# One block of every 16-step turn fetched by SP, row by row: a GRU over a projected embedding table

## The chip, the cores and the metric

The kernel runs on one core of one Trainium2 chip. The metric is the device time of one execution in microseconds (us). Three runs of the kernel before took 1089.58, 1090.4 and 1093.35 us; the median is 1090.4 us. The engines of the core are named as in the profile: PE (TensorE, matrix products and transposes), PEld (its weight loads), DVE (VectorE), ACT (ScalarE), POOL (GpSimd) and SP (SyncE, here used to issue DMAs). Each engine has its own instruction queue, and they wait for each other through semaphores.

## The reference

A batch of 512 sequences of 200 item numbers goes through a gated recurrent unit with 128 hidden features, and the last state is classified into 100 classes:

```
x   = emb[item_seq]                      # emb: 12500 x 128, float32
mx  = x_t @ W + b_i ;  mh = h @ U + b_r  # W, U: 128 x 384
z   = sigmoid(mx[:, :D] + mh[:, :D])
r   = sigmoid(mx[:, D:2D] + mh[:, D:2D])
hh  = tanh(mx[:, 2D:] + r * mh[:, 2D:])
h   = where(item_seq_t != 0, z*h + (1-z)*hh, h)     # 200 steps in order
y   = softmax(h_last @ Wout + bout)
```

Item numbers may lie past the end of the table; they are brought into its rows first.

## The kernel before

**The table.** Since x_t @ W depends on the item alone, the kernel first multiplies the whole embedding table by W and stores the product in HBM as `table`: one row of 384 float32 values (1536 bytes) for each item. It also stores the transposed embedding itself as `rows` (512 bytes each). The last stores of the table are issued by SP (L226 to L230).

**The steps.** The batch is cut into four blocks of 128 sequences. Blocks 0 and 1 form chain 0, blocks 2 and 3 form chain 1; the chains are independent, and PE, ACT and DVE work on them in turn, so that one chain's matrix products lie beside the other's gates. The first 10 steps (`RAW`) use rows of the plain embedding, gathered while the table is still being made. The other 190 steps, numbered n = 0 to 189 (step t is n + 10), use rows of the table.

**The gathers.** For each step and block POOL issues one indirect DMA (L302) that fetches 128 rows of `table` into the arena, a ring of 12 steps in SBUF; the row numbers lie in `row_table` in SBUF, one for each partition. That is 4 gathers a step and 760 in all, written out one after the other. Before a chain's gathers of step n, POOL waits until PE has transposed the rows of step n - 12 out of the same slot (`s_free`).

**PE.** In each table step and chain PE transposes the gathered rows into the gates' sums in PSUM (`transpose_rows`, L377, six transposes), waiting for each block's slot semaphore, and then adds h @ U (L383, L385, L389). DVE's last instruction of a step and chain is L552, which makes the new h. The table steps run in a loop on PE, ACT and DVE whose body is one turn of the ring: with a ring of 12, 15 turns and 10 steps left over.

**SP.** Once the table is stored, SP has nothing to do until the result (L233).

Of the kernel before, what the change touches and what calls it, by code (L numbers as in the profile page):

```python
# [7 lines left out]
I32 = mybir.dt.int32  # L8
# [4 lines left out]
P = 128  # L13
# [2 lines left out]
CHAINS = ((0, 1), (2, 3))  # L16
WIDTH = 2 * P
RAW = 10
RING = 12
CHUNK = 8  # L20
HALF = CHUNK // 2
GROUP = 4
# [1 line left out]
AHEAD = 4  # L24
# [3 lines left out]
def gru(nc: bass.Bass, item_seq, emb_cols, W, U, b_i, b_r, Wout, bout, out):  # L28
# [14 lines left out]
    BATCH, STEPS = item_seq.shape  # L43
# [3 lines left out]
    assert D == P and GATES == 3 * D and BATCH == BLOCKS * P and 1 <= RAW <= RING  # L47
    TURNS = (STEPS - RAW) // RING
    LEFT = STEPS - RAW - TURNS * RING
    BOTH = range(len(CHAINS))  # L50

    TILES = ITEMS // P
# [7 lines left out]
    rows = nc.dram_tensor("rows", [ITEMS + 1 + P, D], F32, kind="Internal").ap()  # L60
    row_tiles = rows[0:TILES * P, :].rearrange("(p j) n -> p j n", j=TILES)
    table = nc.dram_tensor("table", [ITEMS + 1 + P, GATES], F32, kind="Internal").ap()
    table_tiles = table[0:TILES * P, :].rearrange("(p j) n -> p j n", j=TILES)

    with ExitStack() as ctx:
# [3 lines left out]
        def sem(name):  # L69
            return ctx.enter_context(nc.semaphore(name))  # L70

        def per_chain(name):
            return [sem(f"{name}{c}") for c in BOTH]

# [92 lines left out]
        s_padrow = sem("pad_rows_stored")  # L167

        s_slot = [[sem(f"slot{s}_block{k}_gathered") for k in range(BLOCKS)] for s in range(RING)]
        s_x = per_chain("x_turned")  # L170
        s_xT = per_chain("xT_ready")
        s_free = per_chain("rows_transposed")
# [18 lines left out]
        def over_table_steps(eng, one_turn):  # L191
            with eng.Fori(0, TURNS) as turn:
                one_turn(turn, RING)
            one_turn(TURNS, LEFT)

        def columns(i):
            return arena[:, i * P:min((i + 1) * P, ITEMS)]

        @block.sync
        def _(sp):  # L200
            for q in range(CHUNKS):
                sp.dma_start(arena[:, q * CHUNK * P:(q + 1) * CHUNK * P],
                             emb_cols[:, q * CHUNK * P:(q + 1) * CHUNK * P]).then_inc(s_emb[q], 16)
            sp.dma_start(arena[:, CHUNKS * CHUNK * P:ITEMS], emb_cols[:, CHUNKS * CHUNK * P:ITEMS]
                         ).then_inc(s_emb[CHUNKS], 16)

            for q in range(CHUNKS):
                sp.wait_ge(s_tact, q + 1)
                sp.wait_ge(s_tdve, q + 1)
                sp.dma_start(row_tiles[:, q * CHUNK:(q + 1) * CHUNK, :], turned[q % STAGES][:, :, :]  # L210
                             ).then_inc(s_rows[q % STAGES], 16)
            sp.wait_ge(s_tact, CHUNKS + 2)
            sp.wait_ge(s_tdve, CHUNKS + 1)
            sp.dma_start(row_tiles[:, TILES - 1, :], turned_last[:, 0, :]).then_inc(s_rows_last, 16)
            sp.dma_start(rows[TILES * P:ITEMS, :], turned_last[0:REST, 1, :]).then_inc(s_rows_last, 16)
            sp.dma_start(rows[ITEMS + 1:ITEMS + 1 + P, :], turned_last[:, 2, :]).then_inc(s_rows_last, 16)

            for g in range(GROUPS):
                sp.wait_ge(s_pact, (g + 1) * (GROUP // 2))
                sp.wait_ge(s_pdve, (g + 1) * (GROUP // 2))  # L220
                sp.dma_start(table_tiles[:, g * GROUP:(g + 1) * GROUP, :], proj[g % AHEAD][:, :, :]
                             ).then_inc(s_store[g % AHEAD], 16)
            last = proj[GROUPS % AHEAD]
            s_last = s_store[GROUPS % AHEAD]
            sp.wait_ge(s_pact, GROUPS * (GROUP // 2) + 1)
            sp.dma_start(table_tiles[:, TILES - 1, :], last[:, 0, :]).then_inc(s_last, 16)  # L226
            sp.wait_ge(s_pdve, GROUPS * (GROUP // 2) + 1)
            sp.dma_start(table[TILES * P:ITEMS, :], last[0:REST, 1, :]).then_inc(s_last, 16)
            sp.wait_ge(s_pact, GROUPS * (GROUP // 2) + 2)
            sp.dma_start(table[ITEMS + 1:ITEMS + 1 + P, :], last[:, 2, :]).then_inc(s_last, 16)  # L230

            sp.wait_ge(s_prob, 1)
            sp.dma_start(out.rearrange("(k p) n -> p k n", p=P), probs[:, :, :]).then_inc(s_out, 16)  # L233
            sp.wait_ge(s_out, 16)

        @block.gpsimd
        def _(pool):
            pool.memset(ident[:, :], 0.0).then_inc(s_ident0, 1)
            pool.memset(pins[:, :], 0.0).then_inc(s_ident0, 1)
            pool.wait_ge(s_ident0, 1)  # L240
            pool.affine_select(out=ident[:, :], in_=ident[:, :], compare_op=ALU.not_equal, fill=1.0,
                               base=0, pattern=[[-1, P]], channel_multiplier=1).then_inc(s_ident, 1)
            pool.wait_ge(s_ident0, 2)
            pool.affine_select(out=pins[:, :], in_=pins[:, :], compare_op=ALU.not_equal, fill=PINNED,
                               base=0, pattern=[[-1, P]], channel_multiplier=1).then_inc(s_pins, 1)

            pool.iota(copy_i[:, :], pattern=[[1, 1]], base=2, channel_multiplier=1).then_inc(s_copy, 1)
            pool.wait_ge(s_copy, 1)  # L250
            pool.tensor_copy(copy_f[:, :], copy_i[:, :]).then_inc(s_copy, 1)
            pool.wait_ge(s_seq, 16)
            pool.tensor_copy(item_f, seq[:, :, :]).then_inc(s_idx, 1)
            pool.wait_ge(s_idx, 1)
            pool.wait_ge(s_copy, 2)
            pool.tensor_scalar(over_f, item_f, float(ITEMS), copy_f[:, 0:1], ALU.is_ge, ALU.mult
                               ).then_inc(s_copy, 1)
            pool.tensor_scalar(row_f, item_f, 0.0, float(ITEMS), ALU.is_lt, ALU.mult).then_inc(s_idx, 1)
            pool.wait_ge(s_idx, 2)
            pool.tensor_tensor(row_f, row_f, item_f, ALU.add).then_inc(s_idx, 1)  # L260
            pool.tensor_scalar(pad_f, item_f, 0.0, float(ITEMS), ALU.is_equal, ALU.mult).then_inc(s_idx, 1)

            pool.tensor_scalar(masked[:, :].rearrange("p (t k) -> p t k", k=BLOCKS),
                               item_f[:, :, 0:RAW].rearrange("p k t -> p t k"), 0.0, None, ALU.is_equal
                               ).then_inc(s_pins, 1)
            pool.wait_ge(s_idx, 4)
            pool.tensor_scalar(row_f, row_f, 0.0, float(ITEMS - 1), ALU.max, ALU.min).then_inc(s_idx, 1)
            pool.wait_ge(s_idx, 5)
            pool.tensor_tensor(row_f, row_f, pad_f, ALU.add).then_inc(s_idx, 1)
            pool.wait_ge(s_idx, 6)  # L270
            pool.wait_ge(s_copy, 3)
            pool.tensor_tensor(row_f, row_f, over_f, ALU.add).then_inc(s_idx, 1)
            pool.wait_ge(s_idx, 7)
            pool.tensor_copy(row_table[:, :, :], row_f.rearrange("p k t -> p t k")).then_inc(s_idx, 1)
            pool.wait_ge(s_idx, 8)
            pool.wait_ge(s_pins, 2)

            pool.wait_ge(s_padrow, 16 * 2)
            for q in range(STAGES):
                pool.wait_ge(s_rows[q], 16 * len(range(q, CHUNKS, STAGES)))  # L280
            pool.wait_ge(s_rows_last, 16 * 3)
            for t in range(RAW):
                for k in range(BLOCKS):
                    pool.indirect_dma_start(  # L284
                        raw_row(t, k), None, rows,
                        bass.IndirectOffsetOnAxis(row_table[:, t, k:k + 1], 0)
                    ).then_inc(s_slot[t][k], 16)

            for q in range(AHEAD):
                stores = len(range(q, GROUPS, AHEAD)) + (3 if q == GROUPS % AHEAD else 0)  # L290
                pool.wait_ge(s_store[q], 16 * stores)
            for t in range(RAW, STEPS):
                n = t - RAW
                s = n % RING
                for c in BOTH:
                    if n >= RING:

                        pool.wait_ge(s_free[c], n - RING + 1)
                    for k in CHAINS[c]:
                        if n < RAW:  # L300
                            pool.wait_ge(s_slot[n][k], 16)
                        pool.indirect_dma_start(  # L302
                            ring_rows(s, k), None, table,
                            bass.IndirectOffsetOnAxis(row_table[:, t, k:k + 1], 0)
                        ).then_inc(s_slot[s][k], 16)

        @block.tensor
        def _(pe):
# [59 lines left out]
            def transpose_rows(turn, s, c):  # L368

                t = RAW + turn * RING + s  # L370
                for i, k in enumerate(CHAINS[c]):
                    for n, (dst, g) in enumerate(((reset_sum[c], 1), (cand_x[c], 2), (update_sum[c], 0))):
                        if n == 0:
                            pe.wait_ge(s_slot[s][k], turn * 16 + (32 if s < RAW else 16))
                        if n == 2 and i == 0:
                            pe.wait_ge(s_z[c], t)
# [233 lines left out]
```

## Time and profile before

| | before |
|---|---|
| median of three runs | 1090.4 us |
| profiled execution | 1093.43 us |
| its span, first to last instruction | 1091.6 us |
| PE busy | 981.0 us (90%) |
| DVE busy | 862.6 us (79%) |
| POOL busy | 803.7 us (74%) |
| POOL gathers of the table (L302) | 760, 979 ns each |
| granted TensorE clock, mean | 0.991 |

The span is the time between the first and the last instruction of the profiled execution; 1.8 us of its own time lie around it, and it took 3.0 us more than the median of the runs. Busy times of engines add up to more than the span, since the engines work side by side. "Idle before" is the time an engine stood still just before an instruction, and what ended that is inferred from semaphore events, so it can be named wrongly.

### The profile page before, as it was taken

To read this page: it belongs to the slowest core of one execution; us is meant where nothing else is said; L and a number is where in the kernel's file an instruction comes from. 1 tells how busy PE (TensorE), PEld (TensorE's weight loads), DVE (VectorE), ACT (ScalarE), POOL (GpSimd) and SP (SyncE) were. 2 spreads that over 40 slices of the span, in tenths; PEclk is the share of its full clock that TensorE was granted. 3 is DMA by queue.
4 is the path that set the end of the run, shared out by engine and by line. 5 is a ranking of instruction groups with operands and counts; after the bars stand their busy time and mean duration, and the time that the engine had idled before them with its cause. 6 is when DMAs were issued, how large, how long until landed. Compare 5 with 4: busy or idle time off the path is not lost.

```text
span 1091.6 us, 15880 instructions
## 1 busy us (share of the span) xinstructions
PE 981.0 (90%) x5185; PEld 756.4 (69%) x5185; DVE 862.6 (79%) x2074; ACT 577.7 (53%) x1288; POOL 803.7 (74%) x820
## 2 busy tenths in 40 slices
PE   6899999999999999999999999888888888888885
PEld 5556887777777777777777776666666666666664
DVE  3344778888888888888888888888888888888886
ACT  3334655555555555555555555555555555555554
POOL 6574777777777777777777777777777777777773
PEclk9899999999999999999999999999999999999998
DMA  9997555555555555555555555555555555555552
GB/s 359 378 360 262 159 157 153 153 152 154 151 155 152 153 153 153 154 152 152 153 156 152 153 152 154 153 152 151 154 152 155 153 153 154 153 152 154 152 155 81
DMA packets 59696, 185.75 MB, mean 170 GB/s; under 512 B 14830, under 2 KB 16408, under 8 KB 59672
## 3 DMA queue, kind: packets, MB, share of 16 engines
q0 software_dynamic: 49920, 152.09, 49.4%
q1 hardware_dynamic: 8356, 32.47, 7.5%
q10 hardware_dynamic: 1396, 0.91, 0.3%
q8 instruction: 9, 0.15, 0.1%
q14 instruction: 15, 0.12, 0.0%
HBM read 159.35 MB, written 26.07 MB: 170 GB/s over the span
## 4 chain that ended last, share of the span: by engine, by line
DVE 29%; DMA 23%; PE 16%; issue 12%; ACT 11%; POOL 9%; DVEq 0%; SPq 0%; POOLq 0%; ACTq 0%
DMA arena<-table,row_table 21%; ACT cand L482 10%; DVE rh L541 10%; POOL arena L302 9%; DVE zc L549 9%; DVE pre L544 9%; PE bank L318 5%; PE bank L377 4%; DMA rows<-turned 1%; PE bank L383 1%; DVE h L552 1%; PE bank L389 1%; PE bank L385 1%; PE bank L358 1%; PE bank L362 1%
## 5 line engine op out<-in xcount | busy, mean ns | idle before, releaser
L302 POOL DMA_INDIRECT arena<-table,row_table x760 | 744.4, 979 | 241.0 <-issue 178.2
L377 PE MATMUL bank<-ident,arena 128*128 128x128 f32 x2280 | 346.5, 277 | 64.3 <-DMA arena<-table,row_table 63.9
L377 PEld LDWEIGHTS bank<-ident,arena 128*128 128x128 f32 x2280 | 269.4, 141 | 141.6 <-DMA arena<-table,row_table 103.0
L482 ACT ACTIVATE cand<-pre,bi 128x256 f32<-128x256 f32 x400 | 203.3, 508 | 280.4 <-DVE pre L544 280.4
L383 PE MATMUL bank<-h,U_sb 128*128 128x256 f32 x800 | 261.6, 409 | 22.5 <-DVE h L552 4.9
L549 DVE SCALAR_TENSOR_TENSOR zc<-z,cand 128x256 f32<-128x256 f32 x400 | 171.2, 428 | 92.9 <-ACT cand L482 92.9
L389 PE MATMUL bank<-h,U_sb 128*128 128x256 f32 x800 | 239.3, 381 | 0.0
L385 PE MATMUL bank<-h,U_sb 128*128 128x256 f32 x800 | 238.6, 380 | 0.0
L478 ACT ACTIVATE r<-bank,b_gates 128x256 f32<-128x256 f32 x400 | 185.1, 463 | 83.3 <-PE bank L383 82.2
L541 DVE SCALAR_TENSOR_TENSOR rh<-bank,br,r 128x256 f32<-128x256 f32 x400 | 191.8, 479 | 44.6 <-ACT r L478 34.2
L480 ACT ACTIVATE z<-bank,b_gates 128x256 f32<-128x256 f32 x400 | 189.3, 473 | 69.8 <-PE bank L389 69.8
L552 DVE TENSOR_TENSOR h<-zh,zc 128x256 f32<-128x256 f32 x400 | 172.9, 432 | 13.8
L544 DVE TENSOR_TENSOR pre<-rh,bank 128x256 f32<-128x256 f32 x400 | 168.2, 420 | 13.8
L383 PEld LDWEIGHTS bank<-h,U_sb 128*128 128x128 f32 x800 | 120.1, 190 | 74.0 <-DVE h L552 73.9
L546 DVE TENSOR_TENSOR zh<-z,h 128x256 f32<-128x256 f32 x400 | 169.7, 424 | 0.4 <-ACT z L480 0.4
L385 PEld LDWEIGHTS bank<-h,U_sb 128*128 128x128 f32 x800 | 152.4, 190 | 20.7
L389 PEld LDWEIGHTS bank<-h,U_sb 128*128 128x128 f32 x800 | 137.3, 190 | 37.6 <-DVE pre L544 3.1
L318 PE MATMUL bank<-W_sb,arena 128*128 128x384 f32 x198 | 70.5, 510 | 3.7 <-ACT proj L453 3.7
L318 PEld LDWEIGHTS bank<-W_sb,arena 128*128 128x128 f32 x198 | 38.6, 201 | 28.5 <-ACT proj L453 4.4
L517 DVE COPY proj<-bank 128x384 f32<-128x384 f32 (+1 forms) x49 | 27.2, 557 | 39.0 <-PE bank L318 33.7
L284 POOL DMA_INDIRECT raw<-rows,row_table x40 | 38.0, 950 | 20.2 <-issue 11.9
L453 ACT COPY proj<-bank 128x384 f32<-128x384 f32 x50 | 23.8, 479 | 45.0 <-PE bank L318 39.1
(55 smaller groups left out, 165.8 us busy)
## 6 DMA issues: line engine op xcount, KB each, us to landing
table<-proj SPq DMA_DIRECT2D x24, 768.0 KB, 3.9
arena<-table,row_table POOLq DMA_INDIRECT x760, 3.1
arena<-in_L_rec_emb SPq DMA_DIRECT2D x12, 512.0 KB, 10.1
rows<-turned SPq DMA_DIRECT2D x12, 512.0 KB, 10.7
raw<-rows,row_table POOLq DMA_INDIRECT x40, 4.0
seq<-in_r_item_seq ACTq DMA_DIRECT2D x1, 400.0 KB, 10.3
table<-proj SPq DMA_DIRECT2D x2, 192.0 KB
out_probs<-probs SPq DMA_DIRECT2D x1, 200.0 KB, 2.6
```

The lines of the kernel that those rows point to most:

```text
L302: pool.indirect_dma_start(ring_rows(s, k), None, table, bass.IndirectOffsetOnAxis(row_table[:, t, k:k + 1], 0)).then_inc(s_slot[s][k], 16)
L377: last = pe.matmul(dst[:, i * P:(i + 1) * P], ring_row(s, k, g), ident[:, :], start=(i == 0), stop=False, is_transpose=True, skip_group_ch ...
L383: pe.matmul(reset_sum[c], U_sb[:, D:2 * D], h[c][:, :], start=False, stop=True, skip_group_check=True).then_inc(s_reset[c], 1)
L385: pe.matmul(cand_h[c], U_sb[:, 2 * D:3 * D], h[c][:, :], start=False, stop=True, skip_group_check=True).then_inc(s_cand[c], 1)
L389: pe.matmul(update_sum[c], U_sb[:, 0:D], h[c][:, :], start=False, stop=True, skip_group_check=True).then_inc(s_update[c], 1)
L478: act.activation(r[c][:, :], reset_sum[c], ACT.Sigmoid, bias=b_gates[:, 1:2]).then_inc(s_r[c], 1)
L480: act.activation(z[c][:, :], update_sum[c], ACT.Sigmoid, bias=b_gates[:, 0:1]).then_inc(s_z[c], 1)
L482: act.activation(cand[c][:, :], pre[c][:, :], ACT.Tanh, bias=bi[:, 2:3]).then_inc(s_tanh[c], 1)
L541: dve.scalar_tensor_tensor(out=rh[c][:, :], in0=cand_h[c], scalar=br[:, 2:3], in1=r[c][:, :], op0=ALU.add, op1=ALU.mult).then_inc(s_rh[c], 1)
L544: dve.tensor_tensor(pre[c][:, :], rh[c][:, :], cand_x[c], ALU.add).then_inc(s_pre[c], 1)
L549: dve.scalar_tensor_tensor(out=zc[c][:, :], in0=z[c][:, :], scalar=1.0, in1=cand[c][:, :], op0=ALU.subtract, op1=ALU.mult).then_inc(s_zc[c ...
L552: dve.tensor_tensor(h[c][:, :], zh[c][:, :], zc[c][:, :], ALU.subtract).then_inc(s_h[c], 1)
```

## The change

The ring gets 16 steps instead of 12, so the loop has 11 turns and 14 steps left over. In each turn, and in the steps left over, block 3 of the ring's step 12 is no longer gathered by POOL: POOL skips it, 12 gathers in all. SP fetches these rows instead, with 128 one-row DMAs a turn, whose source address is taken from a register. The row numbers of these 12 blocks are first stored from SBUF to a small table in HBM (`slow_rows`); SP loads them into 32 registers at a time, four times a block. The fetch of turn 0 begins once the table is stored; that of a later turn waits, after its first register load, until PE has transposed the same slot's rows of the turn before. PE waits for the 128 DMAs with a semaphore of their own (`s_slow`).

```diff
-RING = 12
+RING = 16
+SLOW_STEP = 12
+SLOW_BLOCK = 3
+BATCH_ROWS = 32
...
+            sp.wait_ge(s_idx, 8)
+            with nc.allow_non_contiguous_dma("a column of row numbers for each turn, written once"):
+                sp.dma_start(slow_rows.rearrange("n p -> p n"),
+                             row_table[:, RAW + SLOW_STEP:STEPS:RING, SLOW_BLOCK]).then_inc(s_slow_rows, 16)
+            sp.wait_ge(s_slow_rows, 16)
+            for q in range(AHEAD):
+                sp.wait_ge(s_store[q], 16 * table_stores(q))
+            sp.wait_ge(s_padrow, 16 * 2)
+            row = [ctx.enter_context(sp.register(f"row{i}")) for i in range(BATCH_ROWS)]
+
+            def slow_block(turn):
+                for first in range(0, P, BATCH_ROWS):
+                    sp.load(row, slow_rows[bass.ds(turn, 1), first:first + BATCH_ROWS])
+                    if first == 0 and not isinstance(turn, int):
+                        sp.wait_ge(s_free[1], (turn - 1) * RING + SLOW_STEP + 1)
+                    for i in range(BATCH_ROWS):
+                        p = first + i
+                        sp.dma_start(ring_rows(SLOW_STEP, SLOW_BLOCK)[p:p + 1, :],
+                                     table[bass.ds(sp.snap(row[i], min_val=0, max_val=ITEMS + P), 1), :]
+                                     ).then_inc(s_slow, 16)
+
+            slow_block(0)
+            with sp.Fori(1, TURNS + 1) as turn:
+                slow_block(turn)
...
                     for k in CHAINS[c]:
+                        if (s, k) == (SLOW_STEP, SLOW_BLOCK):
+                            continue
...
-                        if n == 0:
+                        if n == 0 and (s, k) == (SLOW_STEP, SLOW_BLOCK):
+                            pe.wait_ge(s_slow, (turn + 1) * (P * 16))
+                        elif n == 0:
                             pe.wait_ge(s_slot[s][k], turn * 16 + (32 if s < RAW else 16))
```

## Rows read from the trace of the kernel before

**Rows 1.** The page: busy time by engine; shares of the chain by engine.
```profile
PE 981.0 (90%) x5185; PEld 756.4 (69%) x5185; DVE 862.6 (79%) x2074; ACT 577.7 (53%) x1288; POOL 803.7 (74%) x820
...
DVE 29%; DMA 23%; PE 16%; issue 12%; ACT 11%; POOL 9%; DVEq 0%; SPq 0%; POOLq 0%; ACTq 0%
```

**Rows 2.** L552 by windows: stretch, length, busy (count), clock, DMA share, GB/s.
```profile
206.50:626.30 419.80, 78.63 (x180) 1.00 0.54 153
...
673.00:1032.20 359.20, 59.50 (x140) 1.00 0.54 153
```

**Rows 3.** Waits, 110 to 655 us: line, releaser, total us, times, longest.
```profile
POOL arena L302 <- issue: 123.1, 404, 0.3
...
POOL arena L302 <- PE bank L377: 6.4, 21, 0.3
```

**Rows 4.** Waits between 670 and 1065 us.
```profile
PEld bank L377 <- DMA arena<-table,row_table: 98.7, 158, 1.0
...
POOL arena L302 <- issue: 49.1, 161, 0.3
POOL arena L302 <- PE bank L377: 44.8, 147, 0.3
```

**Rows 5.** Timeline of POOL: first and last table gather (start, duration).
```profile
99.88 0.95 POOL L302 DMA_INDIRECT arena<-table,row_table  x1 [9.79 <-DMA table<-proj]
...
1074.58 0.95 POOL L302 DMA_INDIRECT arena<-table,row_table  x1 [0.30 <-issue]
```

**Rows 6.** Timeline of DVE: h of chain 0, steps 20, 22, 199.
```profile
206.72 0.48 DVE L552 TENSOR_TENSOR h<-zh,zc 128x256 f32<-128x256 f32 x1
...
216.28 0.42 DVE L552 TENSOR_TENSOR h<-zh,zc 128x256 f32<-128x256 f32 x1
...
1081.29 0.43 DVE L552 TENSOR_TENSOR h<-zh,zc 128x256 f32<-128x256 f32 x1
```

**Rows 7.** Waits of SP's DMA queue: the longest.
```profile
SPq L233 <- DVE probs L579: 991.2, 1, 991.2
```

**Rows 8.** Line L302: its gathers' time from issue to landing.
```profile
DMA to landing us min/median/max: 2.9/3.1/4.8
```

**Rows 9.** Timeline: SP's 13 loads in a row, ACT's two one-row stores.
```profile
0.72 6.27 SPq L202 DMA_DIRECT2D arena<-in_L_rec_emb  x12
...
4.68 0.58 ACTq L445 DMA_DIRECT2D rows<-pad_raw  x1
...
5.29 0.23 ACTq L446 DMA_DIRECT2D table<-pad_row  x1
...
7.04 0.46 SPq L204 DMA_DIRECT2D arena<-in_L_rec_emb  x1
```

**Rows 10.** Lines L210, L221, L228: SP's issue times (ns min/median/max).
```profile
L210 SPq DMA_DIRECT2D rows<-turned x12: 319/320/641, 7.9 to 32.2; - x12
...
L221 SPq DMA_DIRECT2D table<-proj x24: 319/320/1176, 34.9 to 94.6; - x24
...
L228 SPq DMA_DIRECT2D table<-proj x1: 716/716/716, 95.9 to 95.9; - x1
```

**Rows 11.** The page: DMA issues, KB each and us to landing.
```profile
arena<-in_L_rec_emb SPq DMA_DIRECT2D x12, 512.0 KB, 10.1
...
br<-in_L_rec_b_r ACTq DMA_DIRECT2D x1, 1.5 KB, 12.8
```

**Rows 12.** The page: the gathers' queue, packets, MB, share of 16 engines.
```profile
q0 software_dynamic: 49920, 152.09, 49.4%
```

**Rows 13.** The page: table gathers and raw gathers, count, busy us, mean ns.
```profile
L302 POOL DMA_INDIRECT arena<-table,row_table x760 | 744.4, 979 | 241.0 <-issue 178.2
...
L284 POOL DMA_INDIRECT raw<-rows,row_table x40 | 38.0, 950 | 20.2 <-issue 11.9
```

More of the change, by code:

```diff
@@ L49, in gru @@
     LEFT = STEPS - RAW - TURNS * RING
+    assert RAW <= SLOW_STEP < LEFT
     BOTH = range(len(CHAINS))
@@ L62, in gru @@
     table = nc.dram_tensor("table", [ITEMS + 1 + P, GATES], F32, kind="Internal").ap()
+    slow_rows = nc.dram_tensor("slow_rows", [TURNS + 1, P], I32, kind="Internal").ap()
     table_tiles = table[0:TILES * P, :].rearrange("(p j) n -> p j n", j=TILES)
@@ L169, in gru @@
         s_slot = [[sem(f"slot{s}_block{k}_gathered") for k in range(BLOCKS)] for s in range(RING)]
+        s_slow_rows = sem("slow_rows_stored")
+        s_slow = sem("slow_rows_fetched")
         s_x = per_chain("x_turned")
@@ L194, in over_table_steps, with table_stores @@
             one_turn(TURNS, LEFT)
+        def table_stores(q):
+            return len(range(q, GROUPS, AHEAD)) + (3 if q == GROUPS % AHEAD else 0)
         def columns(i):
@@ L289, in _ @@
             for q in range(AHEAD):
-                stores = len(range(q, GROUPS, AHEAD)) + (3 if q == GROUPS % AHEAD else 0)
-                pool.wait_ge(s_store[q], 16 * stores)
+                pool.wait_ge(s_store[q], 16 * table_stores(q))
             for t in range(RAW, STEPS):
```

## The prediction

> **What bounds the kernel now.** I read the page's busy times first: PE leads with 90% and POOL has only 74%, yet the chain of waits, followed back from the end, gives PE 16% and DMA, "issue" and POOL together 44% [rows 1]. Such shares are a mean over stages, so I cut the span into stretches and counted DVE's last instruction of a step, L552, which runs twice a step. From 206.5 to 626.3 us it runs 180 times, which is 90 steps at 419.8/90 = 4.664 us; from 673.0 to 1032.2 us 140 times, 70 steps at 359.2/70 = 5.131 us [rows 2]. Nothing in the loop differs between the two, so the limit does. In the first stretch no wait of PE for a gather is among the listed ones [rows 3]; in the second PE waits 98.7 us for gathers, 158 times [rows 4].
>
> POOL shows the other side. Its first table gather starts at 99.88 us and its last, the 760th, at 1074.58 us [rows 5]: (1074.58 - 99.88)/759 = 1.284 us a gather, hence 4 x 1.284 = 5.137 us a step, the pace of the second stretch. One trap stands in the waits: some of POOL's idle time is put down to PE, as if the ring were full. But 6.4/21 = 0.305 us and 44.8/147 = 0.305 us are the same as its plain issue gaps, 123.1/404 = 0.305 us [rows 3, 4]. It is always the same gap, and POOL never waits for a slot. So POOL issues without a break from 99.88 us to the end, slower than PE, ACT and DVE can go. They have a head start, since their first 10 steps need no table row and POOL gathers ahead meanwhile; they use it up at 4.664 against 5.137 us a step and catch up in the mid-600s. From there POOL's count of gathers sets the end.
>
> **What POOL loses.** 12 of 760 gathers go, one a turn in 11 turns and one in the 14 steps left over (step 12 of them), all before the last gather: 12 x 1.284 = 15.4 us. What follows the last gather's start, 1091.6 - 1074.58 = 17.0 us [rows 5], is unchanged: the last step has no SP block. Span 1091.6 - 15.4 = 1076.2 us.
>
> What is late next? The steps alone: h of step 20 at 206.72 us and 179 steps of 4.664 us give step 199 at 1041.6 us; in the trace it is at 1081.29 us, 10.3 us ahead of the end [rows 6], so the engines' own limit would be 1051.9 us. POOL still ends 24.3 us later, and that margin pays for small delays of PE. The switch of pace moves later by the same reasoning, to about step 144, and the late pace to (63 x 1.284)/16 = 5.06 us.
>
> **What SP gains.** SP is idle for 991.2 us, in a wait for the result [rows 7]; nothing but the output's DMA is queued behind its new work, and that comes after the last block anyway. What SP must keep is a rhythm. PE's transposes of a slow block free its slot; SP then issues 128 DMAs; PE needs them 16 steps later, and while it waits, the products of chain 1 (and soon both chains, PE works in order) stand behind that wait. Call S the time from one such release to the next if SP alone sets it. The first is step n = 12, t = 22; with h of that step at 216.28 us [rows 6] the release is about 215.5 us. Eleven turns later is n = 188, the last step but one: a step of 4.7 us and the usual 12.7 us from the last landing to the end (the 17.0 us less 0.95 issue, 0.3 gap and 3.1 landing [rows 5, 8]) follow. So SP's end is 215.5 + 11 S + 17.4 = 233 + 11 S. It stays below POOL's 1076.2 us for S up to 76.7 us, and equals the kernel before at S = 78.1 us. Above that each us of S costs 11 us.
>
> S = 128 c + 3 L + the larger of L and D. c is one row's DMA with its register work, L a load of 32 registers (the first of a block's four is issued ahead of the wait and lies beside D), D the last landing and PE's transposes: 3.1 us [rows 8] and 0.8, about 4.
>
> No register load, register arithmetic or register-addressed DMA stands in this trace's views, so c and L are bounded. The issue itself: ACT's two one-row stores took 0.23 and 0.58 us [rows 9]; SP's 36 big ones have a median of 0.32 us when it isn't pressed, one of 84 rows 0.72 [rows 10]. I take 0.32, the nearest in engine and between the two one-row times. The gap to the next instruction: in SP's 13 loads in a row, which start 6.32/12 = 0.527 us apart, the last begins 0.05 us after the end of the one before [rows 9]. The register work: between 0 and POOL's issue gap of 0.305; I take two instructions of one gap each, 0.10. So c is 0.47 us, and lies between 0.28 (0.23 + 0.05) and 0.93 (0.58 + 0.05 + 0.30). L lies between 0 and a gather's whole round trip, 3.1 us [rows 8], if the registers come together; I take 2. S = 60.2 + 6 + 4 = 70 us, 6.5 us inside the limit; by the low ends 39.8, by the high ends 132, which would be 233 + 1452 = 1685 us. The limit falls where c is 0.52 at my L.
>
> Here a rule of the Trainium skill speaks against the change. Its page Runtime: NRT & Kernel Launch, section Instruction fetch mechanics, says that a register load from HBM costs about 200 ns for each register, even in bulk. Then L is 6.4 us, S 60.2 + 19.2 + 6.4 = 85.8 us and the span 1177 us, where by my L it is 1076. No row here shows such a load.
>
> A second price is one for each DMA, not for its issue. A gather lands 3.1 us after its issue, but the next begins 1.28 us after it [rows 5, 8]: landing lies beside the next issue, so I charge it once a block. The Trainium skill's page DMA: Bandwidth & Descriptors, section Anatomy of one DMA, gives each DMA a fixed 2.0 us; paid one after another it would make S 256 + 10 = 266 us and the span 3160 us. The gathers' rows say that it overlaps, and I give the serial reading under 1 in 100.
>
> **The rest of the edits at nothing, with their cover.** The store of the 12 x 128 row numbers stands on SP's queue behind the table's last stores; the smallest pieces of this trace (12 bytes each) took 12.8 us to land in the first rush [rows 11]. SP starts its first block some 103 to 113 us in, and it isn't needed before 215.5: 30 us of cover even at S = 70. Were POOL's first gather to wait for that store, up to 12 us would be lost one for one; it waits for earlier ones. The 16-step ring gives POOL slots it never lacked. Fewer and longer loop bodies touch PE, ACT and DVE, covered by 24.3 us, or 2.2 us a turn. One-row packets share the DMA engines, which are half idle: the gathers take 49.4% [rows 12]; a gather that lands at 4.8 us in place of 3.1 [rows 8] delays the end once, by 1.7 us.
>
> **Rivals.**
> (a) SP's issue is too slow, the other side. If register-addressed one-row DMAs go at the pitch of SP's unbroken run, 0.527 us, and 0.10 comes on top, c is 0.63 and S = 80.3 + 6 + 4 = 90 us: 233 + 993 = 1226 us. It decides from S = 78. For it: that run is the only one of SP without waits between; against it: those moved 512 KB each [rows 11], and the second one-row store took 0.23 us.
> (b) The 32 registers of a load come one by one. Priced at the shortest issue of the trace, 0.23 us each, L is 7.3 us, S = 60.2 + 21.9 + 7.3 = 89 us: 233 + 983 = 1216 us. The skill's rule above is this mechanism. For it: a load names 32 registers; against it: nothing measured here.
> (c) No change that can be told. S falls within 77.8 to 78.4, or POOL's pitch grows by 2% beside SP's DMAs and eats the 15.4 us: 1091 us. Against the latter: POOL's 40 raw gathers, beside SP's table stores, took 950 ns each, the later ones 979 [rows 13].
>
> **How the numbers follow.** The profiled execution took 1093.4 us, 1.8 over its span and 3.0 over the median; taking the saving off the median, 1090.4 - 15.4 = 1075.0 us. The likeliest case's own range is 1071 to 1079. Chances: forecast 0.66 (in it 0.04 for an S of 77 that leaves a part), (a) 0.18, (b) 0.10, (c) 0.06. A measurement of this kernel can tell about 0.3% (3.3 us) from no change. That makes faster 0.66, same 0.06, slower 0.28. The range over all reaches from 1070 up to 1135, S = 82, which takes in the milder part of (a) and (b) and leaves out the rest, some 0.19.
>
> **What would show it.** Right: 748 gathers still 1.28 us apart, the last starting near 1059; the late pace near 5.06 us; PE's waits still for gathers, hardly any for SP's block; SP waiting for PE at each turn's start. Wrong: SP never waiting, its DMAs over 0.52 us apart, or loads of 4 us and more; then PE waits once a turn for SP, and POOL runs far ahead and waits for slots.

## The result, and the profile after

The change makes the kernel 1.1% slower: 1102.7 us (median; 1098.6 to 1105.5) against 1090.0 us before, a ratio of 1.0107 with a 95% interval of 1.0069 to 1.0145. I had forecast 1075.0 us, and my range reached from 1070 to 1135. The saving on POOL's side came: it issues 748 gathers in place of 760, 1.286 us apart, and the last starts 13 us earlier, at 1061.6 us in place of 1074.6 [rows 5]. The line of the gathers after (duration in ns, first and last start):

```profile
L339 POOL DMA_INDIRECT arena<-table,row_table x748: 942/946/1196, 100.9 to 1061.6; - x187
```

But POOL no longer sets the end.

The profiled execution took 1105.5 us, its span 1103.3. First the page's busy times, and the shares of the chain of waits, which answer to [rows 1].

```profile
PE 995.2 (90%) x5185; PEld 764.6 (69%) x5185; DVE 854.4 (77%) x2074; ACT 549.7 (50%) x1288; POOL 793.4 (72%) x808
...
SPq 60%; issue 20%; PE 12%; DVE 4%; DMA 2%; ACT 2%; DVEq 0%; ACTq 0%
```

Busy times differ little. The chain does: SP's queue, absent from it before, holds 60%. The waits of the whole kernel after (line and releaser, total us, times, longest) answer to [rows 4]:

```profile
POOL arena L339 <- issue: 217.0, 712, 0.3
...
PEld bank L416 <- DMA arena<-table: 50.9, 10, 6.7
PE bank L416 <- DMA arena<-table: 48.6, 10, 6.5
...
POOL arena L339 <- PE bank L416: 10.7, 35, 0.3
```

Before, PE waited some 160 times for gathers, at most 1.0 us each in the late stretch. Now no wait of PE for a gather of POOL is among the listed ones; it waits ten times, 5 us each, for SP's block (here the source is `table` alone, without `row_table`). And SP waits for PE, in its DMA queue's waits, once:

```profile
SPq L261 <- PE bank L416: 27.2, 1, 27.2
```

That is the second block, which waits for the slot of the first. After it SP never waits for PE again. In the timeline of SP (start, length, line, count) the eleven blocks from there on stand as one row:

```profile
212.67 870.93 SPq L260 DMA_DIRECT2D arena<-table  x1408
```

The first of them takes 71 us from its first row to its last, and the ten others, each with what stands before it, 80.0 us: (870.9 - 71)/10. From block start to block start the mean is 80.1 us. PE, where nothing held it up, needed 16 x 4.664 = 74.6 us for 16 steps [rows 2]. Here is what fills the 80 us. The lines of SP's loop after, with duration in ns (min/median/max), first and last start:

```profile
L255 SPq TENSOR_LOAD <-slow_rows x48: 3717/4020/5117, 107.6 to 1066.2; - x48
L255 SPq TENSOR_LOAD <-slow_rows_ptr x44: 1091/1330/1696, 179.9 to 1064.9; - x44
...
L260 SPq MOVE arena<-table x1536: 29/29/38, 112.9 to 1083.3; - x192
L260 SPq DMA_DIRECT2D arena<-table x1536: 224/225/320, 113.0 to 1083.4; - x192
...
L261 SPq FUSED_REGOPS  x1536: 44/44/59, 112.8 to 1083.2; - x192
```

A row costs a one-row DMA of 225 ns and two register instructions of 44 and 29 ns; with the gaps between them a row follows the last after 0.417 us. That is the median; one row in some 40 comes 0.3 us later, so the mean is 0.425 us, 54.4 us for 128. A load of 32 registers takes 4.0 us, and in the loop, where the turn's number is a register, each is preceded by a second load of 1.3 us, from `slow_rows_ptr`, which I take to be the address of `slow_rows`. The chain of waits through one end of a turn, in order of time (start, us, what), shows that these lie one behind the other, with the jump back to the loop's start as "issue":

```profile
443.66 3.26 issue
...
447.00 1.64 SPq L255
...
448.84 3.85 SPq L255
...
452.99 0.27 SPq L260
```

and those through a load inside the block:

```profile
466.51 1.42 SPq L255
...
468.13 4.15 SPq L255
```

With pointer, arithmetic and gaps a load adds 5.6 us in the mean (5.9 us is what I first read, and what the expectations below use together with 53.4 us for the rows). The jump, with its own instructions, takes what is left, some 3.3 us: 54.4 + 4 x 5.6 + 3.3 = 80.1 us.

### The profile page after: what moved, and what is told of

Its sections match the earlier page's. It is cut to its first block, busy times and chain, and to the rows that moved or that the text cites. A ratio compares the mean times of both kernels' runs of the same rounds, so it can differ in the third digit from the quotient of the medians.

```text
span 1103.3 us, 20660 instructions
## 1 busy us (share of the span) xinstructions
PE 995.2 (90%) x5185; PEld 764.6 (69%) x5185; DVE 854.4 (77%) x2074; ACT 549.7 (50%) x1288; POOL 793.4 (72%) x808
## 4 chain that ended last, share of the span: by engine, by line
SPq 60%; issue 20%; PE 12%; DVE 4%; DMA 2%; ACT 2%; DVEq 0%; ACTq 0%
SPq L260 33%; SPq L255 21%; SPq L261 6%; PE bank L355 5%; DMA rows<-turned 1%; ACT cand L521 1%; DVE rh L580 1%; DVE zc L588 1%; DVE pre L583 1%; PE bank L422 1%; PE bank L424 1%; PE bank L428 1%; PE bank L395 1%; PE bank L399 1%; PE bank L396 1%
## 5 line engine op out<-in xcount | busy, mean ns | idle before, releaser
L339 POOL DMA_INDIRECT arena<-table,row_table x748 | 734.1, 981 | 238.7 <-issue 217.0
L416 PE MATMUL bank<-ident,arena 128*128 128x128 f32 x2280 | 319.1, 276 | 48.6 <-DMA arena<-table 48.6
L416 PEld LDWEIGHTS bank<-ident,arena 128*128 128x128 f32 x2280 | 277.0, 143 | 91.1 <-DMA arena<-table 50.9
L422 PE MATMUL bank<-h,U_sb 128*128 128x256 f32 x800 | 278.6, 430 | 34.8 <-DVE h L591 7.3
L428 PE MATMUL bank<-h,U_sb 128*128 128x256 f32 x800 | 242.7, 385 | 1.0 <-DVE pre L583 0.4
L424 PE MATMUL bank<-h,U_sb 128*128 128x256 f32 x800 | 242.1, 385 | 0.0
```

The source lines that it names most:

```text
L339: pool.indirect_dma_start(ring_rows(s, k), None, table, bass.IndirectOffsetOnAxis(row_table[:, t, k:k + 1], 0)).then_inc(s_slot[s][k], 16)
L416: last = pe.matmul(dst[:, i * P:(i + 1) * P], ring_row(s, k, g), ident[:, :], start=(i == 0), stop=False, is_transpose=True, skip_group_ch ...
L422: pe.matmul(reset_sum[c], U_sb[:, D:2 * D], h[c][:, :], start=False, stop=True, skip_group_check=True).then_inc(s_reset[c], 1)
L424: pe.matmul(cand_h[c], U_sb[:, 2 * D:3 * D], h[c][:, :], start=False, stop=True, skip_group_check=True).then_inc(s_cand[c], 1)
L428: pe.matmul(update_sum[c], U_sb[:, 0:D], h[c][:, :], start=False, stop=True, skip_group_check=True).then_inc(s_update[c], 1)
```

## The experiments

**The ring alone.** `RING = 16` in the kernel before, nothing else.

```diff
-RING = 12
+RING = 16
```

> Part of the change alone: the ring of 16 steps, and POOL still gathers all 760 blocks. Theory (SP's fetch cycle of 80.0 us a turn sets the end of the changed kernel): the ring costs nothing, the time is that of before, 1090 us within 3. Rival (the longer loop bodies or the wider ring cost by themselves): about 1100 us, and the pace of the steps before POOL is caught up with is over 4.66 us.

Measured: 1091.1 us, ratio 1.0004 (0.9992 to 1.0016). No cost or gain of the ring is to be seen.

**The loads taken out.**

```diff
             def slow_block(turn):
-                    sp.load(row, slow_rows[bass.ds(turn, 1), first:first + BATCH_ROWS])
...
+            sp.load(row, slow_rows[0:1, 0:BATCH_ROWS])
             slow_block(0)
```

> The changed kernel, but the 32 registers are loaded once, ahead of the first block; the 1536 one-row DMAs stay, so SP's blocks hold rows of turn 0 (that part of the computation is changed). Theory (the four register loads a turn, 5.9 us each with what follows them, are what is too much): SP's turn falls to 128 x 0.417 + 3 = 56 us, below the 74.6 us that PE takes for 16 steps; SP waits for PE in every turn, POOL sets the end again, and the span is that of POOL's 748 gathers, about 1077 us (1074 to 1080). Rival (the one-row DMAs themselves, their landing or their load on the DMA engines): it stays at 1095 to 1103 us. Rival (the granted clock, 0.971 in the changed kernel, is a cause and not an effect): the clock stays under 0.98 and the time above 1085.

Measured: 1076.1 us, ratio 0.9866 (0.9847 to 0.9884), granted clock 0.994. The same 1536 DMAs, and the kernel is as fast as forecast: neither their issue nor their load on the DMA engines is the cause by itself, and the clock's fall to 0.971 was an effect: it went with the loads. SP now waits for PE in each of eleven turns:

```profile
SPq L260 <- PE bank L416: 237.3, 11, 46.7
```

**The loop written out.**

```diff
-            with sp.Fori(1, TURNS + 1) as turn:
+            for turn in range(1, TURNS + 1):
                 slow_block(turn)
```

> The changed kernel with SP's loop written out: each turn's number is a constant, so no pointer is loaded ahead of each register load and there is no jump back. Theory: a load of 32 registers stays at the 4.1 us that block 0 shows, SP's turn is 53.4 + 4 x 4.2 = 70 us, under 74.6, and POOL sets the end: about 1077 us. Rival (the load's cost is the 32 registers whatever the loop, and enough to hold SP above 76.7 us a turn): 1090 us or more. Rival (written-out code must be fetched as it runs and is slower): SP's pitch from row to row above 0.45 us and the span above 1085.

Measured: 1076.3 us, ratio 0.9875 (0.9851 to 0.9900). The 48 loads keep their price, the 44 pointer loads are gone, and so is the jump. The load's line:

```profile
L255 SPq TENSOR_LOAD <-slow_rows x48: 3806/4152/4422, 106.9 to 1025.6; - x48
```

SP's own waits:

```profile
SPq L261 <- PE bank L416: 84.1, 11, 29.8
```

and the waits of the whole kernel:

```profile
PEld bank L416 <- DMA arena<-table,row_table: 77.5, 126, 2.0
```

SP waits in all eleven turns and PE waits for POOL's gathers again: POOL sets the end. The register loads as such can stay: SP's own turn is some 71 us here (54.4 + 4 x 4.2), 9 us less than in the changed kernel, and that is enough.

**Each load twice.** The load's line was doubled.

```diff
                     sp.load(row, slow_rows[bass.ds(turn, 1), first:first + BATCH_ROWS])
+                    sp.load(row, slow_rows[bass.ds(turn, 1), first:first + BATCH_ROWS])
```

> The changed kernel with every register load done twice. Theory: 4 more loads of some 5.6 us make SP's turn 102 us, and each turn's excess stands whole on the path: 3 more in the first turn and 4 in each of ten, 1103 + 16.8 + 224 = 1344 us. Rival (loads lie mostly beside something else, and another wait sets the turn of 80 us): under 1200 us.

Measured: 1144.9 us, ratio 1.0497 (1.0466 to 1.0528), far from 1344. The trace says why: the first of the two loads, whose registers are written again before they are read, doesn't stand in the compiled program. Only its pointer load remains:

```profile
L255 SPq TENSOR_LOAD <-slow_rows_ptr x44: 993/1270/1558, 177.7 to 1102.4; - x44
...
L256 SPq TENSOR_LOAD <-slow_rows x48: 3438/3983/4457, 106.8 to 1104.6; - x48
L256 SPq TENSOR_LOAD <-slow_rows_ptr x44: 820/961/1152, 179.1 to 1103.7; - x44
```

So the run doubled the pointer loads alone, four more of some 1 us a turn. SP's turn in its trace is 83.8 us (mean of ten), 3.7 more, and the span 1141.1 us, 37.8 more: 10.2 us for each us of the turn. The expectation fell through the edit, not through the theory; the rival's "under 1200" can't claim it, since the loads weren't doubled.

**Sixteen registers a load.** `BATCH_ROWS` 16 in place of 32.

> The changed kernel with 16 registers a load instead of 32: eight loads a block instead of four, the same 128 registers. Theory A (the 4.0 us of a load are its 32 registers, read one after the other at some 0.125 us): a load of 16 takes 2.0 us, only pointer, arithmetic and row start are paid eight times; SP's turn is 53.4 + 8 x 3.9 + 3 = 88 us and the span 1103 + 10.2 x 8 = 1185 us. Theory B (a load is one round trip of 4.0 us whatever it brings): 53.4 + 8 x 5.9 + 3 = 104 us and 1103 + 10.2 x 24 = 1348 us.

Measured: 1174.1 us, ratio 1.0776 (1.0738 to 1.0813).

```profile
L255 SPq TENSOR_LOAD <-slow_rows x96: 1870/2106/2621, 104.7 to 1141.9; - x96
```

Half the registers, half the time (2.1 against 4.0 us): the time of a load goes by its registers, 4.02/32 = 0.126 us each, as if they came one after the other. Theory A holds and B is out. For loads of a few registers no run shows this; the pointer load's 1.3 us would be ten of them. SP's turn is 86.3 us, the span 1170.0: (1170.0 - 1103.3)/(86.3 - 80.1) = 10.8 us for each us.

**The row numbers in SBUF, the loop kept.** After the store to HBM one more DMA brings the numbers back into 12 partitions of a small tile.

```diff
+            sp.dma_start(slow_sb[0:TURNS + 1, :], slow_rows).then_inc(s_slow_sb, 16)
+            sp.wait_ge(s_slow_sb, 16)
...
-                    sp.load(row, slow_rows[bass.ds(turn, 1), first:first + BATCH_ROWS])
+                    sp.load(row, bass.at_runtime_partition(slow_sb[0:1, first:first + BATCH_ROWS], turn))
```

> The changed kernel with the row numbers brought back from HBM once into 12 partitions of SBUF, from where SP loads its registers; the loop stays. Theory: no pointer is loaded (1.3 us less a load) and a register read from SBUF costs no more than one from HBM: SP's turn is at most 53.4 + 4 x 4.4 + 3 = 74 us, under 76.7, and POOL sets the end, 1077 us. Rival (a read of SBUF is as slow as pointer and load together, or slower): SP's turn stays at 80 us and the time near 1103 us.

Measured: 1076.2 us, ratio 0.9857 (0.9824 to 0.9890).

```profile
L259 SPq TENSOR_LOAD <-slow_sb x48: 2028/2064/2133, 109.9 to 1021.2; - x48
```

32 registers from SBUF take 2.06 us, half of what they take from HBM, and no pointer load stands on the line.

**The time filled with DMAs instead.** The written-out loop, with 24 more one-row DMAs a block into a spare tile.

```diff
+EXTRA = 24
...
+                    for i in range(EXTRA // (P // BATCH_ROWS)):
+                        p = first + i
+                        sp.dma_start(spare[p:p + 1, :],
+                                     table[bass.ds(sp.snap(row[i], min_val=0, max_val=ITEMS + P), 1), :]
+                                     ).then_inc(s_slow, 16)
...
-                            pe.wait_ge(s_slow, (turn + 1) * (P * 16))
+                            pe.wait_ge(s_slow, (turn + 1) * ((P + EXTRA) * 16))
```

> The written-out SP loop (no pointer loads, no jump), with 24 more one-row DMAs a block, into a spare tile: the loads' excess is gone, and about as much time is filled with DMAs instead. Theory (only the length of SP's turn counts, whatever fills it): the turn is 152 x 0.417 + 4 x 4.2 = 80.3 us, again over the limit of 76.7, and the span near 1110 us: the first release at 212, 76 us for the first block, ten turns of 80.3, and 19.6 to the end. Rival (register loads harm the other engines by themselves, through HBM or the granted clock): 1077 us, as without the 24.

Measured: 1120.8 us, ratio 1.0262 (1.0236 to 1.0289). In SP's timeline a block starts at 210.31 and the next at 291.94, 81.6 us later:

```profile
210.31 13.50 SPq L262 DMA_DIRECT2D arena<-table  x32
...
291.94 4.01 SPq L262 DMA_DIRECT2D arena<-table  x10
```

The mean of the ten turns is 81.3 us. That is 1 us more than reckoned, which at 10 to 11 us for each is the 10 us by which the time is over the expectation. Loads or DMAs, it is the length of SP's turn that counts.

**Twelve in place of 24**, to try the limit of 76.7 us.

```diff
-EXTRA = 24
+EXTRA = 12
```

> The written-out SP loop with 12 more one-row DMAs a block into a spare tile, in place of 24. Theory (SP's turn costs nothing up to 76.7 us, since PE then falls behind by less than POOL's later start of the limit): the turn is 80.8 - 12 x 0.417 = 76.0 us, PE waits 1.3 us a turn for SP and the time is still that of POOL's 748 gathers, 1076 us (1074 to 1081). Rival (each us over PE's own 74.6 us counts): 1076 + 11 x 1.4 = 1091 us.

Measured: 1076.7 us, ratio 0.9865 (0.9844 to 0.9886). The first blocks start 75.7 and 76.5 us apart, and the mean of the first eight turns is 76.0 us:

```profile
210.48 13.49 SPq L262 DMA_DIRECT2D arena<-table  x32
...
286.15 13.50 SPq L262 DMA_DIRECT2D arena<-table  x32
...
362.60 7.33 SPq L262 DMA_DIRECT2D arena<-table  x18
```

SP is late in most turns, since it waits for PE in only three:

```profile
SPq L263 <- PE bank L423: 34.2, 3, 25.6
```

PE loses a us or two a turn, and it costs nothing. Five us more, in the run before, cost 44. So a turn 4 us shorter than that of the changed kernel is short enough.

**A version meant to be faster.** Written out, numbers read from SBUF as ready offsets, a ring of 13 and 14 blocks for SP.

```diff
-RING = 16
-SLOW_STEP = 12
+RING = 13
+SLOW_STEP = 10
...
+            flat = table.rearrange("r g -> (r g)").unsqueeze(0)
...
-                    sp.load(row, slow_rows[bass.ds(turn, 1), first:first + BATCH_ROWS])
+                    sp.load(row, slow_sb[turn:turn + 1, first:first + BATCH_ROWS])
...
-                                     table[bass.ds(sp.snap(row[i], min_val=0, max_val=ITEMS + P), 1), :]
+                                     flat[:, bass.ds(sp.snap(row[i], min_val=0, max_val=(ITEMS + P) * GATES), GATES)]
...
+            pool.tensor_scalar(slow_off[:, 0:SLOW], row_table[:, RAW + SLOW_STEP:STEPS:RING, SLOW_BLOCK], GATES, None, ALU.mult
```

> A version meant to be faster: SP's loop written out, row numbers read from SBUF (2.06 us for 32 registers) as ready offsets, which leaves less register work a row, and a ring of 13 steps, so that 14 blocks go to SP instead of 12. Theory: SP's turn is 128 x 0.36 + 4 x 2.1 = 54 us, under the 60.6 us of 13 steps; POOL issues 746 gathers and the time is 1091 - 14 x 1.284 = 1073 us. Rival (register work a row does not fall): 128 x 0.417 + 8.4 = 61.8 us a turn, at the edge, and 1073 to 1076 us.

Measured: 1074.5 us, ratio 0.9847 (0.9829 to 0.9864). The rival was right on the register work: the arithmetic got only 9 ns shorter (35 against 44), and both instructions stayed.

```profile
L269 SPq FUSED_REGOPS  x1792: 35/35/50, 113.3 to 1007.4; - x200
```

In SP's timeline the 13 blocks after the first stand as one row:

```profile
203.41 804.35 SPq L268 DMA_DIRECT2D arena<-table  x1664
```

The last takes some 60 us, so a turn is (804.4 - 60)/12 = 62 us, over the 60.6 of 13 steps. PE waits for both sides, SP's block and POOL's gathers:

```profile
PEld bank L426 <- DMA arena<-table: 26.3, 12, 3.2
PEld bank L426 <- DMA arena<-table,row_table: 24.7, 42, 1.9
```

The interval overlaps those of the written-out and the SBUF version, so it isn't shown to be faster than they are; all three beat the kernel before by 1.3 to 1.5%.

## Why the prediction was wrong

What held. The bound was read rightly: POOL's pitch set the end, POOL's idle time put down to PE was no wait for a slot, and each gather taken away is worth nearly its 1.28 us once SP keeps up: four versions came to 1076.1 to 1076.7 us, 14 to 15 us under the kernel before in their own runs, where the forecast was 1075.0 and 15.4. The form of SP's limit held too. Above it every us of the turn costs 10 to 11 us (11 by my formula), whatever fills it, and a mean of 76.0 us cost nothing where 81.3 cost 44, which fits the limit of 76.7 us. That a block's first load can't hide once SP is late was in the formula as well.

What failed is the term S, 70 us by the prediction and 80.1 measured:

| part of SP's turn | predicted | measured |
|---|---|---|
| 128 rows | 128 x 0.47 = 60.2 | 128 x 0.425 = 54.4 |
| four loads, and landing | 3 x 2 + 4 = 10 | 4 x 5.6 = 22.4 |
| jump to the loop's start | 0 | 3.3 |
| sum | 70.2 | 80.1 |

The step that failed is L: "L lies between 0 and a gather's whole round trip, 3.1 us [rows 8], if the registers come together; I take 2". They don't come together: the load took 4.0 us, and with its pointer 5.6, so the upper end itself was too low, and a gather's landing was the wrong row for it. The mechanism was in part my rival (b), to which I gave 0.10. Its price of 0.23 us a register was too high (0.126 measured), and it fell short elsewhere: in these programs a load from the table in HBM at a register's place brought a pointer load of 1.3 us with it, though it is a single line of the kernel. The registers alone would not have lost: in the written-out loop each load still takes 4.2 us, the turn is 71 us and the forecast comes out. That the 71 lies so near my 70 is luck, since c was too high by nearly as much as the loads were too low. What carried the turn over the limit is the pointer loads and the jump together. The jump I had not counted for SP at all; "fewer and longer loop bodies" spoke only of PE, ACT and DVE, while SP got a loop it had not had. The excess over the limit was 3.4 us by my 76.7, and some 2.7 by what was lost: the span lies 28.5 us above that of the run with twelve more rows (1074.8), at 10 to 11 us for each us of the turn. The pointer loads (four of 1.3 us and their arithmetic) are more than either. The jump, some 3.3 us, lies between, and no run took out one of the two and nothing else.

The Trainium skill's page Runtime: NRT & Kernel Launch, section Instruction fetch mechanics, had the sign right where I leaned the other way: it says some 200 ns for each register in bulk, these runs show 126 ns from HBM and 64 ns from SBUF (2.06/32) in loads of 32. The same section says that a taken branch to a page which isn't at hand must fetch it first; the 3 us at SP's jump fit that, but no run here took the jump apart.

My rival (a), issue too slow, was wrong: issuing a register-addressed one-row DMA takes 225 ns, as ACT's second one-row store did (0.23 us) [rows 9], and its landing lies beside the next ones: the last row was issued at 1083.4 us, and PE, which waited for it, went on at 1084.7, while rows are issued 0.42 us apart. From S = 80.1 the formula 233 + 11 S gives 1114 us, not 1103: the first block waits for PE, so its first load and the jump are hidden (9 us), and the release comes at 212.5, not 215.5; the tail is some 2 us longer. One sign of being wrong did not come: POOL was to run far ahead and wait for slots, but its idle time put down to PE is again the gap of 0.3 us (10.7/35). Its 63 gathers of 1.286 us make 81.0 us a turn, no faster than SP's 80.

I had the right rivals with too little weight on them: the range held the time, but the point at which SP decides lay 6.5 us from my sum of a turn whose largest unknown, the loads, had no row in the trace.

## What to carry to other kernels

Work that moves to an idle engine has a rhythm to keep: write down its whole turn, loads, pointer loads and the jump included, against the time until the next one is due, since what is over is paid in every turn and what is under costs nothing. An operation that no row shows should be bounded from what it does (here 32 words read, at a price for each), not from the nearest transfer, and where the margin is smaller than that unknown, the forecast hangs on it. If registers must feed DMAs, keep the numbers in SBUF, or write the loop out so that their places are constant: here either turned a loss of 1.1% into a gain of 1.3 to 1.4%.

## What the runs showed of the hardware

After a long stall of PE the granted clock was down for a while. When PE had stood still for 4.3 us in a turn of the changed kernel, the granted clock was 0.52 for the next 3.2 us, mostly the lower of its two levels (1.2 GHz), and then 1.00 again. The windows (stretch, length, busy and count of PE, PEld, DVE, ACT and POOL, clock, DMA share, GB/s):

```profile
361.00:366.00 5.00, 0.83 (x6) 0.49 (x4) 2.99 (x8) 1.52 (x4) 3.78 (x5) 1.00 0.54 157
366.40:369.60 3.20, 3.20 (x12) 2.56 (x11) 0.90 (x2) 0.84 (x2) 2.38 (x3) 0.52 0.53 154
370.00:374.00 4.00, 4.00 (x27) 3.60 (x26) 3.34 (x9) 2.35 (x6) 3.09 (x4) 1.00 0.58 162
```

Waits of up to 1.0 us between gathers, in the kernel before, left the clock at 1.00 [rows 2, 4]. Of the ten stalls of the changed kernel nine (4.1 to 6.5 us) went with such a stretch, of 3 to 7 us; after the one of 3.1 us, which ended at 924.9 us, the clock stayed at 1.00. The slow stretches lay inside SP's turn, and as SP waited for PE in none of these turns, they can have cost time only behind the last block.
